# A mixture-of-experts stage rebuilt: gate rows gathered with the tokens, the sum done by the scatter, products issued early

## The chip, the cores and the metric

One core of a Trainium2 chip runs the whole program. The metric is the device time in microseconds, the median of several runs; one further execution is recorded by the hardware profiler, and all rows below come from it. Engines: TensorE (PE; weight loads are PEld), VectorE (DVE), ScalarE (ACT), GpSimd (POOL) and the DMA queue of SyncE (SP). GpSimd issues the indirect DMAs, which gather or scatter rows by an index in SBUF.

## What is computed

A block with two halves over x of shape (2, 2048, 256), all float32. The first half is a layer norm, linear attention with 16 heads and a gated residual; the change touches none of it but a store. The second is a top-2 mixture of 8 experts:

```python
h = layernorm(x) * (1 + cb) + sb
probs = softmax(h @ router_w.T)                 # 4096 tokens, 8 experts
topw, topi = top_k(probs, 2); topw /= topw.sum() + 1e-6
# each expert keeps the 640 tokens with the largest weight
g, u = disp[e] @ wg[e], disp[e] @ wu[e]         # (640,256) @ (256,1024)
eo = (silu(g) * u) @ wd[e]                      # (640,1024) @ (1024,256)
out = x + gb[b] * scatter_add(eo * weight)      # gb: a gate row of 256 for each of 2 batches
```

## The kernel before

**Precision.** Each float32 operand of the expert products is split into a high half (rounded to fp32r) and a low half (the rest), and each product is three TensorE passes: high x high, high x low, low x high. ScalarE casts the high half of the weights (`split_high`, L644), GpSimd subtracts it for the low half (`split_low`, L508, one block f of 768 columns at a time).

**Attention part** (to about 237 us). SP stores the layer-normed rows h2 to `h2_rows` in DRAM and x with its attention to `out`.

**Routing** (to about 309 us). `choose` finds the two experts and the weights `wgt`, in two parts, and builds `val`: the weight where an expert is chosen, weight minus one elsewhere. A search on the bits of `val` finds each expert's threshold, then slots are counted. For each expert a one-hot product on TensorE (`look`) turns slots into token numbers.

**Experts.** E = 8 experts run one after the other, e = 0 to 7. Each has 640 tokens in CT = 5 tiles of 128, and 1024 hidden units in FC = 8 blocks f of 128. For block f, `gate_up(f)` on TensorE makes gate and up products in two halves h of 320 tokens (12 products each); ScalarE takes the SiLU (L673), VectorE multiplies by up (L1089, here "hidden(f,h)"), ScalarE casts the high half (L677), VectorE subtracts for the low half (L1092). `down(f)` adds 15 products into the banks 4 to 6. The order on TensorE is gate_up(0), gate_up(1), down(0), gate_up(2), down(1) and so on to gate_up(7), down(6), the look-up of expert e+2, down(7). gate_up(f) in half h waits for hidden(f-1,h), since that frees its bank. At f = 4, 5 and 6 the gathered rows of the next expert are transposed.

Around this run, in each engine's own order:

- VectorE: at the start of e, `weigh(e-1)` (L1070) multiplies the five result tiles by `gw`; `combine` (L1078) adds the gathered old rows `xo` of `out`. At f = 0 to 4 it builds `gw` (L1101), gate row times token weight, with ScalarE's share from L664. At f = 1 `find_tokens(e+1)` writes the index tiles; at f = 2 to 6 `describe_*` prepares the look-up of e+2.
- GpSimd: the scatter of e-1 (each tile waits for `combine`), the splits of f = 6 and 7 of e, the gathers of `xg` for e+1 (five, 1 KB rows of `h2_rows`), the gathers of `xo` for e (five, from `out`), then the splits of f = 0 to 5 of e+1. A program-wide rule is that accesses of `out` follow each other, by the semaphore `sc_d` of landed scatters.
- SP: loads the weights of the next experts in two halves, each when both splits of the blocks before it are done.

Of the kernel before, what the change touches and what calls it, by code (L numbers as in the profile page):

```python
# [26 lines left out]
N = B * T  # L27
# [20 lines left out]
XF = 4  # L48
# [72 lines left out]
def build_program(nc, x, w_qkv, w_out, router, wg, wu, wd, c, wmod, rope, consts, out):  # L121
# [3 lines left out]
    h2_rows = nc.dram_tensor("h2_rows", (N, D), F32, kind="Internal").ap()  # L125
    h2_t = h2_rows.rearrange("(n p) d -> n p d", p=P)
# [3 lines left out]
    with ExitStack() as ctx:  # L130
# [40 lines left out]
        val = sb("val", [P, NT, E])  # L171
# [23 lines left out]
        far = sb("far", [P, CT])  # L195
        g_idx = [sb(f"g_idx{i}", [P, CT], I32) for i in range(2)]
        s_idx = [sb(f"s_idx{i}", [P, CT], I32) for i in range(2)]
        w_slot = sb("w_slot", [P, 3, CT])
        w_b = [sb(f"w_b{i}", [P, B, CT]) for i in range(2)]
# [53 lines left out]
        xg = sb("xg", [P, CT, D])  # L253
# [6 lines left out]
        gw0 = sb("gw0", [P, D])  # L260
        gw = sb("gw", [P, CT, D])
        xo, yo = sb("xo", [P, CT, D]), sb("yo", [P, CT, D])
# [38 lines left out]
        raw_a, raw_b, sp_h, sp_l = sem("raw_a"), sem("raw_b"), sem("sp_h"), sem("sp_l")  # L301
# [3 lines left out]
        y_tile, wb_l, wb_d = sem("y_tile"), sem("wb_l"), sem("wb_d")  # L305
        gw0_d, gw_d, xo_d, ym_d, yo_d, sc_d = (sem(n) for n in ("gw0_d", "gw_d", "xo_d", "ym_d", "yo_d", "sc_d"))
# [7 lines left out]
        def _(sp):  # L314
# [69 lines left out]
            steps(sp, step, ATT)  # L384

# [22 lines left out]
        def _(pool):  # L408
# [81 lines left out]
            pool.wait_ge(r_dve, 3)  # L490
# [23 lines left out]
            def gather(rows, dst, idx, done):  # L514
                for a in range(CT):
                    nc.gpsimd.indirect_dma_start(  # L516
                        out=dst[:, a, :], out_offset=None, in_=rows,
                        in_offset=bass.IndirectOffsetOnAxis(ap=idx[:, a:a + 1], axis=0))\
                        .then_inc(done[a // 2] if isinstance(done, list) else done, 16)

            for i in range(2):
                pool.wait_ge(st_h2[i], NT // 2 * 16)
                pool.wait_ge(st_x2[i], NT // 2 * 16)
            pool.wait_ge(idx_d, 1)
            gather(h2_rows, xg, g_idx[0], ga_d)

            def expert(e, par, last):
                for f in (0, 1):
                    split_low(e, FC - 2 + f, e * FC + FC - 2 + f)
                if last < 1:  # L530
                    wait_apart(pool, idx_d, e + 2, apart)
                    wait_apart(pool, trx_d, e * XG + XG, apart)
                    gather(h2_rows, xg, g_idx[1 - par], ga_d)
                wait_apart(pool, sc_d, e * CT * 16 + 16, apart)
                gather(out_rows, xo, g_idx[par], xo_d)
                if last < 1:
                    for f in range(FC - 2):
                        split_low(e + 1, f, e * FC + FC + f)
                for a in range(CT):
                    wait_apart(pool, yo_d, e * CT + a + 1, apart)  # L540
                    nc.gpsimd.indirect_dma_start(  # L541
                        out=out_rows, out_offset=bass.IndirectOffsetOnAxis(ap=s_idx[par][:, a:a + 1], axis=0),
                        in_=yo[:, a, :], in_offset=None, bounds_check=N - 1, oob_is_err=False).then_inc(sc_d, 16)

            with pool.Fori(0, (E - 2) // 2) as k:
                expert(k * 2, 0, 0)
                expert(k * 2 + 1, 1, 0)
            expert(E - 2, 0, 0.5)
            expert(E - 1, 1, 1)
# [4 lines left out]
        def _(act):  # L554
# [104 lines left out]
            def expert(e, par, last):  # L659
                def gate_weight(a):  # L660
                    wait(act, wb_d, e + 1)
                    if a:
                        wait(act, gw_d, e * CT + a)
                    nc.scalar.activation(gw0[:, :], mod_all[:, 0, 3, :], ACT.Copy, scale=w_b[par][:, 0, a:a + 1])\  # L664
                        .then_inc(gw0_d, 1)

                for f in range(FC):
                    for h in range(2):
                        i = e * 2 * FC + 2 * f + h
                        wait(act, gu_d, i + 1)  # L670
                        if f:
# [3 lines left out]
                        if f >= 2:  # L675
                            wait(act, dn_d, e * FC + f - 1)
                        nc.scalar.copy(hid_h[f % 2][:, h * HCAP:(h + 1) * HCAP], hid[h][:, :]).then_inc(hh_d, 1)  # L677
                    if last < 1 and XF <= f < XF + XG:
# [4 lines left out]
                    elif last < 1:  # L683
                        split_high(e + 1, f - 2, e * FC + FC + f - 2)
                    if f < CT:
                        gate_weight(f)

            with act.Fori(0, (E - 2) // 2) as k:
                expert(k * 2, 0, 0)
                expert(k * 2 + 1, 1, 0)  # L690
            expert(E - 2, 0, 0.5)
            expert(E - 1, 1, 1)


        @block.vector
        def _(dve):
# [70 lines left out]
            def choose(lo, hi):  # L767
# [31 lines left out]
                TT(X[1], X[4], b8(Y[6]), ALU.mult)  # L799
# [127 lines left out]
            def place_masks(part):  # L927
# [3 lines left out]
                for k, op in enumerate((ALU.is_gt, ALU.is_equal)):  # L931
                    ins = TT(mask2[:, k, lo:hi, :].rearrange("p e n -> p n e"), val[:, :, lo:hi], tb, op)
# [86 lines left out]
            def find_tokens(e, par):  # L1019

                lk = chained(fin_l, e * 3)
# [375 lines left out]
```

## Time and profile before

| | |
|---|---|
| Median of 3 runs | 758.37 us (756.48 to 760.09) |
| Span of the profiled execution | 752.9 us |
| Span of it in experts 0 to 7 | 309.3 to 752.9 us |
| Busy: PE, DVE, POOL, ACT | 601.8, 523.0, 417.9, 334.2 us |

The profiled span leaves out what lies around it: the median of the runs is 5.5 us above. In a timeline row the columns are the start (us from the span's start), the time taken (us), the engine, the line of the kernel and the operation, then output and inputs, how many instructions are merged, and in brackets how long the engine was idle before it and what ended that. A row of the chain has start, duration and what the time went to.

### The profile page before, as it was taken

To read this page: it belongs to the slowest core of one execution; us is meant where nothing else is said; L and a number is where in the kernel's file an instruction comes from. 1 tells how busy PE (TensorE), PEld (TensorE's weight loads), DVE (VectorE), ACT (ScalarE), POOL (GpSimd) and SP (SyncE) were. 2 spreads that over 40 slices of the span, in tenths; PEclk is the share of its full clock that TensorE was granted. 3 is DMA by queue.
4 is the path that set the end of the run, shared out by engine and by line. 5 is a ranking of instruction groups with operands and counts; after the bars stand their busy time and mean duration, and the time that the engine had idled before them with its cause. 6 is when DMAs were issued, how large, how long until landed. Compare 5 with 4: busy or idle time off the path is not lost.

```text
span 752.9 us, 14123 instructions
## 1 busy us (share of the span) xinstructions
PE 601.8 (80%) x4041; PEld 557.5 (74%) x4041; DVE 523.0 (69%) x1366; ACT 334.2 (44%) x759; POOL 417.9 (55%) x538
## 2 busy tenths in 40 slices
PE   3999789998982002788989989979979979979993
PEld 2677678886761001788978979969969969979993
DVE  2688899996777877665766766757747757736743
ACT  4577677875443000344334424424434425335440
POOL 6689658786773601254474475474473473563612
PEclk9999999999995555698999999999988999989997
DMA  4322268435550200041241341251242152150101
GB/s 123 109 70 70 90 204 248 151 116 179 182 176 17 84 0 11 26 138 36 87 150 34 97 150 46 84 153 50 69 153 82 37 154 81 39 155 1 46 26 35
DMA packets 80467, 70.68 MB, mean 94 GB/s; under 512 B 8604, under 2 KB 75558, under 8 KB 80424
## 3 DMA queue, kind: packets, MB, share of 16 engines
q1 hardware_dynamic: 74632, 54.44, 23.7%
q0 software_dynamic: 5792, 15.74, 6.5%
q8 instruction: 18, 0.29, 0.2%
q14 instruction: 25, 0.20, 0.1%
HBM read 52.32 MB, written 17.83 MB: 93 GB/s over the span
## 4 chain that ended last, share of the span: by engine, by line
PE 41%; DVE 24%; issue 13%; ACT 5%; POOL 2%; DVEq 1%; DMA 1%; ACTq 0%; SPq 0%; POOLq 0%
PE bank L1329 22%; PE bank L1341 12%; DVE gw L1101 3%; DVE feat L855 2%; PE bank L1287 2%; DVE hit L908 2%; ACT w_h L644 2%; DVE hid L1089 2%; DVE x L874 2%; PE bank L1301 2%; ACT act_g L673 1%; DVE st L876 1%; PE bank L1242 1%; DVE cand L919 1%; DVE yo L1078 1%
## 5 line engine op out<-in xcount | busy, mean ns | idle before, releaser
L1329 PE MATMUL bank<-xT_h,w_h 128*128 128x320 f32 x512 | 166.4, 325 | 20.7 <-DVE hid L1089 18.8
L508 POOL TENSOR_TENSOR w_l<-w_raw,w_h 128x768 fp32r<-128x768 f32 x64 | 120.5, 1901 | 111.2 <-ACT w_h L644 111.1
L1329 PE MATMUL bank<-xT_l,w_h 128*128 128x320 f32 x512 | 164.7, 322 | 2.1 <-issue 2.1
L1329 PE MATMUL bank<-xT_h,w_l 128*128 128x320 f32 x512 | 164.2, 321 | 1.8 <-issue 1.8
L677 ACT CAST hid_h<-hid 128x320 fp32r<-128x320 f32 x128 | 58.9, 460 | 136.4 <-DVE hid L1089 114.0
L1329 PEld LDWEIGHTS bank<-xT_h,w_h 128*128 128x128 f32 x512 | 102.5, 200 | 22.5 <-DVE hid L1089 16.1
L1092 DVE TENSOR_TENSOR hid_l<-hid,hid_h 128x320 fp32r<-128x320 f32 x128 | 67.0, 524 | 70.0 <-ACT hid_h L677 58.5
L673 ACT ACTIVATE act_g<-bank 128x320 f32<-128x320 f32 x128 | 55.4, 432 | 114.3 <-remote 58.3
L1089 DVE TENSOR_TENSOR hid<-act_g,bank 128x320 f32<-128x320 f32 x128 | 61.6, 481 | 61.0 <-ACT act_g L673 60.5
L1329 PEld LDWEIGHTS bank<-xT_l,w_h 128*128 128x128 f32 x512 | 102.5, 200 | 2.0 <-issue 2.0
L1329 PEld LDWEIGHTS bank<-xT_h,w_l 128*128 128x128 f32 x512 | 101.8, 199 | 2.3 <-issue 2.3
L1341 PE MATMUL bank<-w_h,hid_h 128*128 128x256 f32 x320 | 96.4, 301 | 4.2 <-issue 3.5
L1341 PE MATMUL bank<-w_h,hid_l 128*128 128x256 f32 x320 | 94.7, 296 | 3.6 <-issue 3.6
L1341 PE MATMUL bank<-w_l,hid_h 128*128 128x256 f32 x320 | 94.6, 296 | 0.5 <-issue 0.5
L541 POOL DMA_INDIRECT out<-yo,s_idx x40 | 40.0, 1001 | 72.9 <-DVE yo L1078 65.6
L516 POOL DMA_INDIRECT xg<-h_rows,g_idx x40 | 39.2, 980 | 66.3 <-DVE s_idx L1032 44.7
L1101 DVE SCALAR_TENSOR_TENSOR gw<-mod_all,w_b,gw 128x256 f32<-128x256 f32 x40 | 58.6, 1466 | 18.2 <-ACT gw L664 11.0
L1341 PEld LDWEIGHTS bank<-w_h,hid_h 128*128 128x128 f32 x320 | 64.6, 202 | 6.1 <-issue 6.0
L1341 PEld LDWEIGHTS bank<-w_h,hid_l 128*128 128x128 f32 x320 | 64.8, 202 | 3.8 <-issue 3.8
L1341 PEld LDWEIGHTS bank<-w_l,hid_h 128*128 128x128 f32 x320 | 65.2, 204 | 2.2 <-issue 2.2
L480 POOL TENSOR_TENSOR rot<-rot_a,rot_b 128x512 f32<-128x512 f32 x32 | 46.8, 1463 | 15.3 <-DVE rot_b L839 15.3
L1150 PE MATMUL bank<-wqkv_h,hT_h 128*128 128x256 f32 (+1 forms) x128 | 47.3, 369 | 8.3 <-DVE hT_l L846 4.5
(199 smaller groups left out, 1321.7 us busy)
## 6 DMA issues: line engine op xcount, KB each, us to landing
w_raw<-wg SPq DMA_DIRECT2D x32, 256.0 KB, 3.1
w_raw<-wu SPq DMA_DIRECT2D x32, 256.0 KB, 4.4
w_raw<-wd SPq DMA_DIRECT2D x16, 512.0 KB, 5.9
x_in<-x SPq DMA_DIRECT2D x32, 128.0 KB, 2.0
q_store<-qT SPq DMA_DIRECT2D x32, 128.0 KB, 1.7
q_in<-q_store SPq DMA_DIRECT2D x32, 128.0 KB, 2.1
x_re<-x SPq DMA_DIRECT2D x32, 128.0 KB, 2.1
out<-x SPq DMA_DIRECT2D x32, 128.0 KB, 2.0
```

The source lines that it names most:

```text
L480: nc.gpsimd.tensor_tensor(rot[s.par(0)][:, :], rot_a[:, :], rot_b[:, :], ALU.add).then_inc(rope_d, 1)
L508: nc.gpsimd.tensor_tensor(w_l[:, f, :], w_raw[:, f, :], w_h[:, f, :].bitcast(F32), ALU.subtract)\
L516: nc.gpsimd.indirect_dma_start(out=dst[:, a, :], out_offset=None, in_=rows, in_offset=bass.IndirectOffsetOnAxis(ap=idx[:, a:a + 1], axis=0))\
L541: nc.gpsimd.indirect_dma_start(out=out_rows, out_offset=bass.IndirectOffsetOnAxis(ap=s_idx[par][:, a:a + 1], axis=0), in_=yo[:, a, :], in_ ...
L673: nc.scalar.activation(act_g[h][:, :], bank[2 * h][:, 0:HCAP], ACT.Silu).then_inc(silu_d, 1)
L677: nc.scalar.copy(hid_h[f % 2][:, h * HCAP:(h + 1) * HCAP], hid[h][:, :]).then_inc(hh_d, 1)
L1089: V.tensor_tensor(hid[h][:, :], act_g[h][:, :], bank[2 * h + 1][:, 0:HCAP], ALU.mult)\
L1092: V.tensor_tensor(hid_l[f % 2][:, h * HCAP:(h + 1) * HCAP], hid[h][:, :], hid_h[f % 2][:, h * HCAP:(h + 1) * HCAP].bitcast(F32), ALU.subtr ...
L1101: V.scalar_tensor_tensor(gw[:, f, :], mod_all[:, 1, 3, :], w_b[par][:, 1, f:f + 1], gw0[:, :], ALU.mult, ALU.add).then_inc(gw_d, 1)
L1150: ins = MM(out, x[j][:, k, :], w[i][:, k, cols], start=n == 0, stop=n == 3 * KC - 1)
L1329: last = MM(bank[2 * h + m][:, 0:HCAP], W[i][:, f, at:at + P], XT[j][:, k, cols], start=n == 0, stop=n == 3 * KC - 1)
L1341: last = MM(bank[4 + a // 2][:, a % 2 * D:(a % 2 + 1) * D], (hid_h, hid_l)[j][f % 2][:, a * P:(a + 1) * P], W[i][:, f, 4 * P:], start=f == ...
```

## The change

- `h2_rows` becomes twice as wide: a row is the normed token and, behind it, the gate row of its batch. SP writes the gate rows for all tokens with two DMAs behind the attention part. A gather now brings both, 2 KB a row, into `xg`, which is doubled.
- `gw`, ScalarE's scaling and VectorE's gate product go. `weigh` becomes one product of result, token weight and gathered gate row, and stands in block f = 0 in two parts.
- The gathers of `xo` and `combine` go; the scatter adds to `out` in the DMA. Empty slots point to token 0 with weight zero.
- `s_idx` is one tile. `find_targets(e)` at f = 3 on VectorE copies the indices once scatter e-1 has landed.
- GpSimd's order becomes: splits 6 and 7 of e, gather of e+1, scatter of e-1, splits 0 to 5 of e+1.
- TensorE issues gate_up(e+1,0) ahead of down(e,7), and gate_up(e+1,1) behind it; the look-up stands ahead of down(6). On VectorE, find_tokens and the describe steps stand between a hidden product and its low half.
- The `val` array goes; the search works on `wgt`.

```diff
-    h2_rows = nc.dram_tensor("h2_rows", (N, D), F32, kind="Internal").ap()
+    h2_rows = nc.dram_tensor("h2_rows", (N, 2 * D), F32, kind="Internal").ap()
+    gate_t = h2_rows[:, D:].rearrange("(b n p) d -> b p n d", b=B, p=P)
...
             steps(sp, step, ATT)
+            sp.wait_ge(ld_all, 3 * B * 16)
+            for b in range(B):
+                sp.dma_start(gate_t[b], mod_all[:, b, 3, :].unsqueeze(1).to_broadcast([P, TB, D])).then_inc(st_gate, 16)
...
+            def scatter(e):
+                wait_apart(pool, sc_d, e * CT * 16 + 16, apart)
+                for a in range(CT):
+                    wait_apart(pool, ym_d, e * CT + a + 1, apart)
+                    nc.gpsimd.indirect_dma_start(
+                        out=out_rows, out_offset=bass.IndirectOffsetOnAxis(ap=s_idx[:, a:a + 1], axis=0),
+                        in_=yo[:, a, :], in_offset=None, compute_op=ALU.add).then_inc(sc_d, 16)
...
+            def expert(e, par, first=False, last=False):
                 for f in (0, 1):
                     split_low(e, FC - 2 + f, e * FC + FC - 2 + f)
-                if last < 1:
+                if not last:
+                    if not first:
+                        wait_apart(pool, ym_d, e * CT, apart)
                     wait_apart(pool, idx_d, e + 2, apart)
-                    wait_apart(pool, trx_d, e * XG + XG, apart)
-                    gather(h2_rows, xg, g_idx[1 - par], ga_d)
-                wait_apart(pool, sc_d, e * CT * 16 + 16, apart)
-                gather(out_rows, xo, g_idx[par], xo_d)
-                if last < 1:
+                    gather(e + 1, 1 - par)
+                if not first:
+                    scatter(e - 1)
+                if not last:
                     for f in range(FC - 2):
                         split_low(e + 1, f, e * FC + FC + f)
-                for a in range(CT):
-                    wait_apart(pool, yo_d, e * CT + a + 1, apart)
...
-                    if f < CT:
-                        gate_weight(f)
...
-                link(TT(X[7], X[3], X[4], ALU.add))
-                link(TT(wgt[:, lo:hi, :], X[0], X[1], ALU.add))
-                V.tensor_scalar(X[5], X[7], -1.0, None, ALU.add).then_inc(r_dve, 1)
-                dve.wait_ge(r_dve, 1 + 2 * part)
-                TT(val[:, lo:hi, :], wgt[:, lo:hi, :], X[5], ALU.add).then_inc(r_dve, 1)
+                TT(wgt[:, lo:hi, :], X[0], X[1], ALU.add).then_inc(r_dve, 1)
...
+            def find_targets(e, par):
+                wait(dve, sc_d, e * CT * 16 + 16)
+                V.tensor_copy(s_idx[:, :], g_idx[par][:, :])
...
+                    V.scalar_tensor_tensor(yo[:, a, :], bank[4 + a // 2][:, a % 2 * D:(a % 2 + 1) * D],
+                                           w_slot[par][:, a:a + 1], xg[par][:, a, D:], ALU.mult, ALU.mult).then_inc(ym_d, 1)
...
+                for f in range(FC):
+                    hidden(f, 0)
+                    if f == 0 and not first:
+                        weigh(e - 1, 1 - par, 0, 2)
+                    if f == 1 and not last:
+                        find_tokens(e + 1, 1 - par)
+                    if f == 2 and ahead:
+                        describe_tiles(e + 2)
+                    if f == 3:
+                        find_targets(e, par)
+                    if f in (3, 4) and ahead:
+                        describe_facts(e + 2, f - 3)
+                    if f == 5 and ahead:
+                        describe_rows(e + 2, 0)
+                    hidden_low(f, 0)
+                    hidden(f, 1)
+                    if f == 0 and not first:
+                        weigh(e - 1, 1 - par, 2)
...
+            def expert(e, par, last=False, ahead=True):
+                for f in range(2, FC):
+                    gate_up(e, par, f)
+                    if not last and XF <= f < XF + XG:
+                        transpose_x(e + 1, 1 - par, f - XF)
+                    if f == FC - 1 and ahead:
+                        wait(pe, xl_d, e * XG + 2 * XG)
+                        look(e + 2)
+                    down(e, f - 1)
+                if not last:
+                    gate_up(e + 1, 1 - par, 0)
+                down(e, FC - 1)
+                if not last:
+                    gate_up(e + 1, 1 - par, 1)
+                    down(e + 1, 0)
```

## Rows read from the trace of the kernel before

**Rows 1.** The page: busy us of each engine, share of the span, instructions.
```profile
PE 601.8 (80%) x4041; PEld 557.5 (74%) x4041; DVE 523.0 (69%) x1366; ACT 334.2 (44%) x759; POOL 417.9 (55%) x538
```
**Rows 2.** Who waited for whom on PE: total us, times, longest.
```profile
PE bank L1329 <- DVE hid L1089: 18.8, 9, 2.9
```
**Rows 3.** The chain that ended last: start us, us, what.
```profile
336.00 1.68 issue
...
341.92 3.15 PE bank L1341 x14
345.06 4.83 PE bank L1329 x24
...
366.88 1.77 PE bank L1329 x12
...
422.10 1.78 PE bank L1329 x12
...
438.90 5.31 PE bank L1329 x24
...
467.89 3.52 PE bank L1329 x24
471.41 1.79 PE bank L1341 x15
473.21 2.03 PE bank L1287 x32
...
696.86 1.78 PE bank L1329 x12
```
**Rows 4.** Timeline of VectorE in expert 2.
```profile
432.85 4.44 DVE L1101 SCALAR_TENSOR_TENSOR gw<-mod_all,w_b,gw 128x256 f32<-128x256 f32 x1 [0.65 <-ACT gw L664]
...
442.13 0.48 DVE L1101 SCALAR_TENSOR_TENSOR gw<-mod_all,w_b,gw 128x256 f32<-128x256 f32 x1 [0.65 <-ACT gw L664]
...
447.58 0.57 DVE L991 TENSOR_TENSOR facts<-vals,in_tile 128x400 bf16<-128x400 f32 x1
```
**Rows 5.** Timeline of GpSimd in experts 2 and 5.
```profile
433.35 3.65 POOL L508 TENSOR_TENSOR w_l<-w_raw,w_h 128x768 fp32r<-128x768 f32 x2
439.38 0.99 POOL L516 DMA_INDIRECT xg<-h_rows,g_idx  x1 [2.38 <-issue]
...
451.12 0.95 POOL L516 DMA_INDIRECT xo<-out,g_idx  x1 [0.30 <-issue]
...
605.98 0.99 POOL L516 DMA_INDIRECT xg<-h_rows,g_idx  x1 [2.30 <-issue]
```
**Rows 6.** Timeline of ScalarE in experts 2 and 5.
```profile
431.58 0.83 ACT L644 CAST w_h<-w_raw 128x768 fp32r<-128x768 f32 x1
...
453.74 0.44 ACT L673 ACTIVATE act_g<-bank 128x320 f32<-128x320 f32 x1 [6.59 <-remote]
...
620.26 0.44 ACT L673 ACTIVATE act_g<-bank 128x320 f32<-128x320 f32 x1 [6.66 <-remote]
```
**Rows 7.** Busy us by stretch; last three: granted clock, DMA share, GB/s.
```profile
226.00:245.00 19.00, 4.28 (x18) 3.08 (x18) 14.98 (x61) 7.00 (x15) 6.06 (x11) 0.56 0.04 14
440.00:442.00 2.00, 2.00 (x10) 2.00 (x9) 0.95 (x2) 1.51 (x4) 1.39 (x3) 0.50 0.89 242
```
**Rows 8.** Timeline of all engines: the first gathers.
```profile
299.19 0.96 POOL L516 DMA_INDIRECT xg<-h_rows,g_idx  x1 [0.30 <-issue]
...
301.96 1.11 PE L1301 MATMUL bank<-const_sb,xg 128*128 128x128 f32 x4 [2.69 <-DMA xg<-h_rows,g_idx]
```
**Rows 9.** Timeline of VectorE at the end of choose.
```profile
242.12 0.21 DVE L804 TENSOR_TENSOR val<-wgt,big 128x48 f32<-128x48 f32 x1
```
**Rows 10.** Timeline at the end: first and last scatter.
```profile
742.76 1.01 POOL L541 DMA_INDIRECT out<-yo,s_idx  x1 [24.50 <-DVE yo L1078]
...
748.16 0.97 POOL L541 DMA_INDIRECT out<-yo,s_idx  x1 [0.31 <-issue]
```

More of the change, by code:

```diff
@@ L657, in _, with expert @@
                 x_high(0, 0, g, bk=g)
[L659 to L665, printed above, removed]
+            def expert(e, par, first=False, last=False):
                 for f in range(FC):
@@ L670, in expert @@
                         wait(act, gu_d, i + 1)
-                        if f:
+                        if f or not first:
                             wait(act, hid_d, i - 1)
@@ L1097, in expert @@
                     if not last and XF <= f < XF + XG:
                         x_low(e + 1, 1 - par, f - XF)
-                    if f < CT:
-                        wait(dve, gw0_d, e * CT + f + 1)
-                        V.scalar_tensor_tensor(gw[:, f, :], mod_all[:, 1, 3, :], w_b[par][:, 1, f:f + 1], gw0[:, :],
-                                               ALU.mult, ALU.add).then_inc(gw_d, 1)
-                    if f == 1 and not last:
-                        find_tokens(e + 1, 1 - par)
@@ L1105, in expert @@
-                    if f == FC - 1 and not last:
-                        find_weights(e + 1, 1 - par)
-                    if ahead:
-                        if f == 2:
-                            describe_tiles(e + 2)
-                        if f in (3, 4):
-                            describe_facts(e + 2, f - 3)
-                        for part in {3: (0,), 5: (1,), 6: (2, 3)}.get(f, ()):
-                            describe_rows(e + 2, part)
+                    if f == 6 and ahead:
+                        describe_rows(e + 2, 3)
@@ L1256, in _ @@
             steps(pe, step, ATT)
-            pe.wait_ge(r_dve, 4)
-            flat = val[:, :, :].rearrange("p n e -> p (n e)")
+            pe.wait_ge(r_dve, 2)
+            flat = wgt[:, :, :].rearrange("p n e -> p (n e)")
             for k in range(2):
@@ new lines, in gate_up @@
+                wait(pe, sp_l, e * FC + f + 1)
+                if f == 0:
+                    wait(pe, xl_d, e * XG + XG)
+                for h in range(2):
+                    if f or not first:
+                        wait(pe, hid_d, e * 2 * FC + 2 * f + h - 1)
+                    cols = slice(h * HCAP, (h + 1) * HCAP)
+                    for m in range(2):
+                        n = 0
+                        for k in range(KC):
+                            for i, j in PASSES:
+                                at = (2 * m + k) * P
+                                last = MM(bank[2 * h + m][:, 0:HCAP], W[i][:, f, at:at + P], XT[j][:, k, cols],
+                                          start=n == 0, stop=n == 3 * KC - 1)
+                                n += 1
+                    last.then_inc(gu_d, 1)
@@ new lines, in down @@
+            def down(e, f):
+                wait(pe, hh_d, e * 2 * FC + 2 * f + 2)
+                wait(pe, hl_d, e * 2 * FC + 2 * f + 2)
+                if f == 0:
+                    wait(pe, ym_d, e * CT)
+                for a in range(CT):
+                    for n, (i, j) in enumerate(PASSES):
+                        last = MM(bank[4 + a // 2][:, a % 2 * D:(a % 2 + 1) * D],
+                                  (hid_h, hid_l)[j][f % 2][:, a * P:(a + 1) * P], (w_h, w_l)[i][:, f, 4 * P:],
+                                  start=f == 0 and n == 0 and a % 2 == 0, stop=f == FC - 1 and n == 2,
+                                  skip_group_check=True)
+                    if f == FC - 1 and a % 2 == 1:
+                        last.then_inc(y_tile, 1)
+                last.then_inc(dn_d, 1)
@@ L1360, in _ @@
+            gate_up(0, 0, 0, first=True)
+            gate_up(0, 0, 1)
+            down(0, 0)
             with pe.Fori(0, (E - 2) // 2) as k:
-                expert(k * 2, 0, 0)
-                expert(k * 2 + 1, 1, 0)
-            expert(E - 2, 0, 0.5)
-            expert(E - 1, 1, 1)
+                expert(k * 2, 0)
+                expert(k * 2 + 1, 1)
+            expert(E - 2, 0, ahead=False)
+            expert(E - 1, 1, last=True, ahead=False)
 def kernel(L0_attn_x, L0_attn_W_qkv, L0_attn_W_out, L0_ffn_router_w, L0_ffn_wg, L0_ffn_wu, L0_ffn_wd, L0_c, L0_wmod):
```

188 lines of the change are left out of this document (65 added, 123 removed).

## The prediction

> **What bounds the kernel now.** I read the page's busy shares first: TensorE works 80% of the span and nothing else comes near it [rows 1]. The chain of work then gives the clock of the expert stage. Expert 1 opens its first gate/up products at 366.88 and expert 7 at 696.86, so a full expert takes 330.0 / 6 = 55.0 us [rows 3]. What TensorE needs when nothing holds it is in the same view: 3.52 us for 24 gate/up products, 1.79 us for 15 down products, 2.03 us for the look-up [rows 3]. Ten transposes, of which four take 1.11 us while the clock is at half [rows 8], are 1.4 us at full clock at most; I take 1.1, since their ends overlap the next products. That is 8 x 5.31 + 2.03 + 1.1 = 45.7 us. So 9.3 us per expert are lost, in two places.
>
> First, the VectorE product that builds the gate weight for f=1 takes 4.44 us where 0.48 us is usual; it starts at 432.85 and ends when GpSimd's two back-to-back low-half splits end (433.35 + 3.65 = 437.0) [rows 4, 5]. Behind it on VectorE stand find_tokens and the next hidden product, and TensorE waits for that product: 18.8 us in 9 waits over the span, about 2.65 us an expert [rows 2]. After the wait 24 products take 5.31 us, not 3.52, at a granted clock of 0.50 (1.2 of 2.4 GHz): 1.8 us more [rows 3, 7].
>
> Second, at f=4 every engine but GpSimd stands still. ScalarE's SiLU starts at 453.74 after 6.59 us without work, and at 620.26 in expert 5 after 6.66 [rows 6]; in expert 0 TensorE waits and crawls from 336.00 to 341.92 [rows 3]. It ends 14.3 us after the first of ten back-to-back indirect DMAs (five of xg, five of xo) begins, in expert 2 (439.38 to 453.74) as in expert 5 (605.98 to 620.26), and 2.6 us after the last one begins at 451.12 [rows 5, 6]. I read it as something that this burst of ten does, not as the transposes. It costs some 3 us net an expert, with a second stretch at half clock behind it.
>
> **The change part by part.**
> *Gate weights gone.* Five ScalarE scalings (0.5 us each) and five VectorE gate products leave each expert, the 4.44 us one among them. The 2.65 + 1.8 us of the first loss go.
>
> *xo gathers and combine gone, gate rows gathered.* GpSimd issues 5 gathers and 5 scatters an expert instead of 10 and 5: 5 x 1.25 = 6.3 us less on its queue. But gather and scatter now stand in one row, so there is still a burst of ten. The new yo product is VectorE work of 256 columns like the gate product it replaces (0.48 us [rows 4]), five an expert: 5 x 0.45 us once they overlap, bounds 0.40 and 0.48. I take a gather of 2 KB rows at the issue time of one of 1 KB (0.95 us; lower bound the same, upper bound twice that), since it has the same 128 rows.
>
> *The add in the scatter.* Its landing is not in this trace. Lower bound: a plain gather issued at 299.19 releases TensorE at 301.96, 2.8 us [rows 8]. Upper bound: the last scatter is issued at 748.16 and the span ends at 752.9, 4.7 us with the program's end in it [rows 10]. The DMAs are not full at that point, so I take 3.2 us, nearer to the gather.
>
> *The new wait.* find_targets(e) stands on VectorE at f=3, behind hidden(3,0), and waits until scatter(e-1) has landed. Behind it wait the low half of (3,0) and hidden(3,1), and for that TensorE's second half of gate_up(4). When does scatter(e-1) land? Count from T, the end of the first half of gate_up(e,0):
> - TensorE without stalls: other half 1.76, down(e-1,7) 1.8, gate_up(1) 3.52, so gate_up(1) ends at T+7.1; gate_up(2) runs 8.9 to 12.4, gate_up(3) 14.2 to 17.7, and the first half of gate_up(4) ends at T+21.3.
> - VectorE: hidden(0,0), two yo products, low half, hidden(0,1) (0.4 to 0.5 us each, the yo products held until down(e-1,7) reaches them) to T+4.4, three yo products to T+5.7, low half, hidden(1,0) to T+6.5. ScalarE's cast for split 6 follows hidden(0,1) by 0.5 us and takes 0.83 [rows 6], so GpSimd's split 6 (half of 3.65, with its end 1.85 us) starts near T+5.7, a tie with the low half. If VectorE wins it, find_tokens meets the split and ends at T+8.5; hidden(1,1) ends at 9.4, the cast for split 7 at 10.7, split 7 at T+12.6. If it loses, everything is 0.8 us later; I add 0.3.
> - The burst: 0.15 us, then 11.74 us between the first and the tenth issue [rows 5], plus 0.15 since scatters go every 1.28 us: the last issue is at T+24.65. Landed at T+27.85.
> - find_targets 0.2, describe_facts 0.5 (0.57 alone [rows 4]), low half 0.45, hidden(3,1) 0.5: TensorE goes on at T+29.5. It stood still for 8 us.
>
> The rest of the expert is 45.7 - 21.3 = 24.4 us, and 2.1 us for the restart at half clock (1.8 was paid after 2.6 us idle; at least that). Period: 29.5 + 24.4 + 2.1 + 0.3 = 56.3 us against 55.0. The stall of the burst lies wholly inside the new wait. Six experts (1 to 6): **+7.8 us**.
>
> The Trainium skill states the rule behind the first loss (SBUF — State Buffer, Who interferes with whom): a VectorE instruction with two SBUF inputs and a GpSimd instruction that reads SBUF exclude each other for the whole instruction. The trace agrees: the gate product, both inputs in SBUF, ended 0.3 us after the splits. By the rule and by the row the sum is the same; by the rule the yo product, with an operand in PSUM, is never held.
>
> *Expert 0* has no wait in find_targets and a burst of five only, which in expert 7 of the kernel before brought no standstill. Gone: the late hidden product (0.6, in the total of [rows 2], and 24 products in 3.79 instead of 3.52), the standstill of 5.9 us less the 1.0 us of work done in it, and what half clock cost behind it: 14 down products 3.15 instead of 1.68 us, gate_up 4.83 instead of 3.52 [rows 3]. Sum **-8.6 us**.
>
> *Expert 7* loses its late product (1.9 us with what follows) but its scatter(6), five issues behind split 7, lands at T+12.75+5.1+3.2 = T+21.1 and gives TensorE 0.7 us of waiting: **-1.2 us**.
>
> *Routing.* The val array goes. In the second part its two last instructions end at 242.33 [rows 9], 0.55 us after wgt would; in the first part it is 1.0 us more, which counts only if the logits are there; together -1.3 us taken (0.6 to 1.6). find_tokens(0) is 0.3 us shorter and the first gathers of 2 KB rows land about 0.3 us later: **-1.3 us**.
>
> *Gate store.* Two DMAs write 4 MB on SP behind the last h2 store. From 226 to 245 the DMAs run at 14 GB/s [rows 7], and the first gather reads these rows after 297; at the 200 to 300 GB/s of busy stretches it is 14 to 20 us. It costs nothing; without that cover it would be those 14 to 20 us.
>
> *Early first products.* gate_up(e+1,0) stands ahead of down(e,7). TensorE did not wait at that place before (the chain runs on at 473.21 and later), so it gives nothing itself; it gives the yo products cover. describe_rows(3) has 2 us to spare before the earlier look-up.
>
> *Tail.* Without combine the first scatter leaves 0.5 us earlier after the last product; five issues go at the same pace (742.76 to 748.16 [rows 10]); the add lands 0.4 to 0.8 us later: **+0.3 us**.
>
> Sum against the profiled span of 752.9: +7.8 - 8.6 - 1.2 - 1.3 + 0.3 = -3.0, a span of 749.9. The median of the runs stands 5.5 us above the span (758.37), so **755.3 us**.
>
> **The rivals.** All turn on the period, and each microsecond in it is six in the time.
> - *The adding scatter is slow (other side).* If it is issued or lands later than a plain one by 1.5 us or more in each expert, by reading the destination before writing it, the wait at f=3 grows by that: taken as 2.7 us an expert it gives 6 x 2.7 + 0.7 in expert 7 = 17 us more, 772 us. It decides from 0.5 us beyond my 3.2: 6 x 0.5 takes the 3.0 us of gain. For it: no row has such a DMA, and find_targets waits for all five. Against: the DMAs are nearly idle then.
> - *The skill's price.* The Trainium skill (DMA: Bandwidth & Descriptors, Latency and other measured facts) puts HBM access at 0.2 us on average and 2 us at high load; one more such trip would give, as an estimate, 0 to 10 us above my time, and this trace has no row for it.
> - *The chain is shorter than I count.* Split 7 a microsecond earlier (find_tokens not caught by split 6), landing at 2.8, restart at 1.7: period 54.5, and 755.3 - 6 x 1.8 = 744 us. For it: the ScalarE queue is 2.5 us lighter. Against: the ten issues are serial and nothing shortens them.
> - *The standstill belongs to the transposes or to the weight load*, not to the burst. Then it stays in expert 0 and comes again after the new wait: 3 to 5 us in seven experts, 780 to 790 us. Against: experts 2 and 5 are freed at the same distance from the burst to 0.1 us, and e = 7, which has a burst of five, shows none.
>
> **How the numbers follow.** Forecast with its own range 748 to 763: 0.45. Slow adding scatter: 0.24. Shorter chain: 0.19. Standstill stays: 0.07. The rest, 0.05, is a slower gather of 2 KB rows (780). Range 742 to 778. A measurement here tells about 0.5% (3.8 us) from no change. Faster by more: half of the forecast's cases and all of the shorter chain, 0.42. Within: the other half less the few of its range that end above, and the mildest slow scatters, 0.26. Slower: 0.32.
>
> **What would show it.** Right: no VectorE product over 2 us at f=1; VectorE idle before find_targets' copy for some 10 us in experts 1 to 6, ended by the scatter's landing; TensorE idle about 8 us before the second half of gate_up(4) there, and none of it in expert 0; period 56.3. Wrong: scatters spaced over 1.3 us or landing over 4 us; down(e,0) or gate_up(2) late because the low half lost to split 6; a standstill at the transposes after the new wait; half clock for longer than some 4 us after each stop.

## The result: 770.9 us, slower than before

| | before | after |
|---|---|---|
| Median of 4 runs | 758.57 us (756.48 to 760.09) | 770.92 us (767.01 to 773.58) |
| Ratio | | 1.0175 (95% interval 1.0132 to 1.0218) |
| Span of the profiled execution | 752.9 us | 770.1 us |
| First gate/up products of experts 0, 1, 6, 7 | 309.3, 366.7, 643.4, 696.7 | 310.1, 357.2, 648.8, 704.5 |
| End of the last product | 741.9 | 754.1 |
| Busy PE, DVE, POOL, ACT | 601.8, 523.0, 417.9, 334.2 | 595.9, 442.3, 400.2, 320.8 |

Every engine has less to do than before, and the kernel is 1.75% slower. The page of the kernel after, busy row (the counterpart of [rows 1]) and the groups that the argument needs:

```profile
PE 595.9 (77%) x4041; PEld 553.7 (72%) x4041; DVE 442.3 (57%) x1248; ACT 320.8 (42%) x717; POOL 400.2 (52%) x498
...
L1323 PE MATMUL bank<-xT_h,w_h 128*128 128x320 f32 x512 | 167.6, 327 | 54.6 <-DVE hid L1073 42.8
...
L528 POOL DMA_INDIRECT out<-yo,s_idx x40 | 62.7, 1568 | 39.0 <-DVE yo L1063 27.3
L518 POOL DMA_INDIRECT xg<-h_rows,g_idx x40 | 39.2, 980 | 50.6 <-DVE g_idx L1023 39.8
```

The late hidden product cost TensorE 18.8 us before [rows 2] and 42.8 us now. The gather of a 2 KB row takes 0.98 us to issue, as one of 1 KB did; the adding scatter 1.57 us, where the plain one took 0.97 [rows 10].

Expert 2 after, which begins at 415.78. GpSimd's timeline, then VectorE's, TensorE's and ScalarE's (the counterparts of [rows 4 to 6]):

```profile
427.71 1.85 POOL L509 TENSOR_TENSOR w_l<-w_raw,w_h 128x768 fp32r<-128x768 f32 x1 [2.53 <-ACT w_h L652]
429.72 1.01 POOL L518 DMA_INDIRECT xg<-h_rows,g_idx  x1
...
436.10 1.63 POOL L528 DMA_INDIRECT out<-yo,s_idx  x1 [0.30 <-issue]
438.03 1.58 POOL L528 DMA_INDIRECT out<-yo,s_idx  x1 [0.30 <-issue]
...
443.65 1.55 POOL L528 DMA_INDIRECT out<-yo,s_idx  x1 [0.30 <-issue]
```

```profile
447.54 0.17 DVE L1028 COPY s_idx<-g_idx 128x5 int32<-128x5 int32 x1 [7.52 <-DMA out<-yo,s_idx]
447.72 0.58 DVE L986 TENSOR_TENSOR facts<-vals,in_tile 128x400 bf16<-128x400 f32 x1
448.21 0.48 DVE L1078 TENSOR_TENSOR hid_l<-hid,hid_h 128x320 fp32r<-128x320 f32 x1
448.62 0.48 DVE L1073 TENSOR_TENSOR hid<-act_g,bank 128x320 f32<-128x320 f32 x1
```

```profile
449.15 0.64 PE L1323 MATMUL bank<-xT_h,w_h 128*128 128x320 f32 x1 [5.96 <-DVE hid L1073]
```

```profile
439.05 0.44 ACT L674 ACTIVATE act_g<-bank 128x320 f32<-128x320 f32 x1 [6.55 <-remote]
```

The ten issues run from 429.72 to 443.65. VectorE's copy of the indices, 0.17 us long, stands from 440 to 447.54 and is released by the last scatter. The copies as a group (the view of one tile):

```profile
who waited for it (us, times):
  DVE s_idx L1028: 55.3, 7
```

TensorE goes on at 449.15, at half clock (windows; the clock is the column behind POOL):

```profile
443.00:449.10 6.10, 0.19 (x1) 0.00 (x0) 1.55 (x4) 0.00 (x0) 3.74 (x3) 0.50 0.39 45
449.10:452.60 3.50, 3.45 (x13) 3.41 (x14) 2.40 (x4) 1.99 (x4) 1.82 (x1) 0.50 0.01 2
452.60:457.00 4.40, 4.40 (x30) 4.40 (x29) 2.12 (x5) 2.12 (x4) 1.50 (x1) 0.81 0.00 0
```

The old stop of ScalarE is still there ("remote", 6.55 us), but in front of the SiLU of block 3. It ends before the copy begins to wait: TensorE stands 2.44 us for the stop and 5.96 us for the copy, and since the copy waits for the landing, at 447.5, the stop adds nothing to the time. In expert 7, the chain:

```profile
725.58 3.77 DMA out<-yo,s_idx
729.35 0.02 issue
729.37 0.04 DVE s_idx L1028
729.41 0.04 issue
729.46 0.48 DVE hid_l L1078
729.94 0.41 DVE hid L1073
```

### The profile page after: what moved, and what is told of

It reads as the page before. It is cut to its first block, busy times and chain, and to the rows that moved or that the text cites. A ratio compares the mean times of both kernels' runs of the same rounds, so it can differ in the third digit from the quotient of the medians.

```text
span 770.1 us, 13880 instructions
## 1 busy us (share of the span) xinstructions
PE 595.9 (77%) x4041; PEld 553.7 (72%) x4041; DVE 442.3 (57%) x1248; ACT 320.8 (42%) x717; POOL 400.2 (52%) x498
## 4 chain that ended last, share of the span: by engine, by line
issue 32%; POOL 19%; DVE 18%; PE 13%; DMA 3%; ACT 1%; DVEq 1%; SPq 1%; POOLq 0%; ACTq 0%
POOL w_l L509 9%; POOL out L528 7%; PE bank L1323 6%; PE bank L1335 3%; POOL xg L518 2%; DVE feat L850 2%; DVE hit L903 2%; DVE x L869 1%; DMA out<-yo,s_idx 1%; DVE st L871 1%; PE bank L1238 1%; DVE cand L914 1%; DVE den_r L856 1%; DMA x_in<-x 1%; DVE hid L1073 1%
## 5 line engine op out<-in xcount | busy, mean ns | idle before, releaser
L509 POOL TENSOR_TENSOR w_l<-w_raw,w_h 128x768 fp32r<-128x768 f32 x64 | 123.4, 1932 | 204.7 <-ACT w_h L652 204.7
L1323 PE MATMUL bank<-xT_h,w_h 128*128 128x320 f32 x512 | 167.6, 327 | 54.6 <-DVE hid L1073 42.8
L1323 PE MATMUL bank<-xT_h,w_l 128*128 128x320 f32 x512 | 166.2, 325 | 0.0
L1335 PE MATMUL bank<-w_h,hid_h 128*128 128x256 f32 x320 | 94.4, 295 | 0.4 <-DVE hid_l L1078 0.4
L1335 PE MATMUL bank<-w_h,hid_l 128*128 128x256 f32 x320 | 91.5, 286 | 1.2 <-issue 1.1
L1335 PE MATMUL bank<-w_l,hid_h 128*128 128x256 f32 x320 | 91.3, 285 | 0.2 <-issue 0.2
L1078 DVE TENSOR_TENSOR hid_l<-hid,hid_h 128x320 fp32r<-128x320 f32 x128 | 63.5, 496 | 35.5 <-ACT hid_h L678 35.5
L528 POOL DMA_INDIRECT out<-yo,s_idx x40 | 62.7, 1568 | 39.0 <-DVE yo L1063 27.3
L1335 PEld LDWEIGHTS bank<-w_h,hid_l 128*128 128x128 f32 x320 | 62.5, 195 | 0.8 <-issue 0.8
L1335 PEld LDWEIGHTS bank<-w_l,hid_h 128*128 128x128 f32 x320 | 62.2, 194 | 1.1 <-issue 1.0
L652 ACT CAST w_h<-w_raw 128x768 fp32r<-128x768 f32 x64 | 52.9, 833 | 0.0
```

The costliest lines, as they stand in the source:

```text
L509: nc.gpsimd.tensor_tensor(w_l[:, f, :], w_raw[:, f, :], w_h[:, f, :].bitcast(F32), ALU.subtract)\
L528: nc.gpsimd.indirect_dma_start(out=out_rows, out_offset=bass.IndirectOffsetOnAxis(ap=s_idx[:, a:a + 1], axis=0), in_=yo[:, a, :], in_offse ...
L652: nc.scalar.copy(w_h[:, f, :], w_raw[:, f, :]).then_inc(sp_h, 1)
L1078: V.tensor_tensor(hid_l[f % 2][:, h * HCAP:(h + 1) * HCAP], hid[h][:, :], hid_h[f % 2][:, h * HCAP:(h + 1) * HCAP].bitcast(F32), ALU.subtr ...
L1323: last = MM(bank[2 * h + m][:, 0:HCAP], W[i][:, f, at:at + P], XT[j][:, k, cols], start=n == 0, stop=n == 3 * KC - 1)
L1335: last = MM(bank[4 + a // 2][:, a % 2 * D:(a % 2 + 1) * D], (hid_h, hid_l)[j][f % 2][:, a * P:(a + 1) * P], (w_h, w_l)[i][:, f, 4 * P:], s ...
```

## The experiments

Twelve kernels, each beside runs of the kernel before on the same chip. That kernel's median was 757.8, 754.0 and 753.7 us in the three groups of four, so between groups the ratios to it are what to compare. The three kernels with an overwriting scatter leave out the add to the old rows of `out` and so compute something else; they are there to price the add.

| kernel | median us | ratio to before (95%) | period of experts 1 to 5, us |
|---|---|---|---|
| after | 770.9 | 1.0175 (1.0132 to 1.0218) | 58.2 to 58.6 |
| two tiles of targets | 725.9 | 0.9575 (0.9540 to 0.9609) | 51.3 to 53.0 |
| scatter that overwrites | 740.0 | 0.9764 (0.9720 to 0.9808) | 53.4 to 54.3 |
| targets found at f = 6 | 727.7 | 0.9613 (0.9575 to 0.9652) | 51.4 to 51.5 |
| two tiles, overwriting scatter | 738.6 | 0.9734 (0.9694 to 0.9774) | 54.2 to 54.5 |
| two tiles, load held | 730.5 | 0.9688 (0.9663 to 0.9713) | 51.2 to 53.9 |
| two tiles, scatters apart | 694.8 | 0.9210 (0.9187 to 0.9233) | 46.6 to 46.7 |
| two tiles, all DMAs apart | **689.8** | 0.9150 (0.9126 to 0.9173) | 45.7 to 45.8 |
| two tiles, late products | 731.8 | 0.9675 (0.9621 to 0.9728) | 52.9 to 54.3 |
| all apart, overwriting scatter | 689.3 | 0.9154 (0.9128 to 0.9181) | 45.7 to 45.8 |
| before, gathers apart | 726.3 | 0.9655 (0.9618 to 0.9692) | 51.4 to 52.3 |
| all apart, late products | 690.7 | 0.9180 (0.9150 to 0.9211) | 45.7 to 45.8 |
| all apart, bounds check | 689.8 | 0.9160 (0.9134 to 0.9187) | 45.7 to 45.8 |

A period is the time from the first gate/up product of one expert to that of the next.

### The wait of find_targets: two tiles, or a later place

```diff
-        s_idx = sb("s_idx", [P, CT], I32)
+        s_idx = [sb(f"s_idx{i}", [P, CT], I32) for i in range(2)]
...
-                wait(dve, sc_d, e * CT * 16 + 16)
-                V.tensor_copy(s_idx[:, :], g_idx[par][:, :])
+                V.tensor_copy(s_idx[par][:, :], g_idx[par][:, :])
```

> The changed kernel with two tiles of scatter targets, so that find_targets(e) waits for nothing and the rest is as it was. Theory (the late landing of the adding scatter reaches TensorE only through this copy): TensorE's 42.8 us of waiting at the second half of gate_up(4) goes, and the stretch at half clock behind it, some 2 us in each of seven experts. Against that stands the stop of ScalarE inside the burst, now hidden behind the wait, which comes back in front of TensorE at 2 to 3 us net in experts 1 to 6. Period 58.3 - 8.3 + 2.5 to 3 = 52.5 to 53, time 732 to 740 us against 770.9. Rival (the burst of ten DMAs holds the engines up by itself, and the copy only happened to stand there): TensorE waits as long for the next SiLU, period over 57, time 760 to 771.

```diff
-                    if f == 3:
-                        find_targets(e, par)
...
-                    if f == 6 and ahead:
-                        describe_rows(e + 2, 3)
+                    if f == 6:
+                        if ahead:
+                            describe_rows(e + 2, 3)
+                        find_targets(e, par)
```

> The changed kernel with find_targets moved from f = 3 to the end of f = 6, still one tile, still waiting for the scatter. The scatter lands some 32 us after gate_up(e,0) begins and block 6 of VectorE comes 12 us or more after that. Theory (place of the wait decides): as with two tiles of targets, within 2 us of its time, 732 to 741 us. Rival (VectorE is too late anyway, or the scatter lands later once nothing holds the experts back): the wait shows again at f = 6, time 745 us or more.

Measured 725.9 and 727.7 us: 45 and 43 us less than the changed kernel, more than I expected, and nearly the same by either edit. So the wait at f = 3 was more than the whole loss, and the place of 0.17 us of work decides some 6% of the time. With the later place a period fell by 7 us in experts 1 to 5, where I had expected 5.5; with two tiles by 7 in experts 1 to 3 and by 5 in 4 and 5.

But it did not fall to the 45.7 us that TensorE needs. Expert 2 with two tiles, which begins at 405.78, ScalarE's, VectorE's and GpSimd's timelines:

```profile
429.84 0.44 ACT L674 ACTIVATE act_g<-bank 128x320 f32<-128x320 f32 x1 [7.34 <-remote]
```

```profile
434.52 4.80 DVE L986 TENSOR_TENSOR facts<-vals,in_tile 128x400 bf16<-128x400 f32 x1
439.25 0.48 DVE L1077 TENSOR_TENSOR hid_l<-hid,hid_h 128x320 fp32r<-128x320 f32 x1
```

```profile
433.64 1.55 POOL L528 DMA_INDIRECT out<-yo,s_idx  x1 [0.30 <-issue]
434.63 4.25 POOL L509 TENSOR_TENSOR w_l<-w_raw,w_h 128x768 fp32r<-128x768 f32 x2
```

Two things remain. ScalarE's SiLU stands 7.34 us: the increment of TensorE's semaphore that frees it is recorded at 429.81, for products that ended near 423.5. TensorE's own products keep their pace until 426.6 and then come with gaps. And a facts product of VectorE takes 4.80 us instead of 0.57, until two low-half splits, which had piled up behind the ten DMAs, are done. The next runs take these apart.

### The add in the scatter

```diff
-                        in_=yo[:, a, :], in_offset=None, compute_op=ALU.add).then_inc(sc_d, 16)
+                        in_=yo[:, a, :], in_offset=None).then_inc(sc_d, 16)
```

> The changed kernel with a scatter that overwrites: the add to the old rows of out is left out, nothing else. Theory (the add makes each scatter dearer to issue and later to land): spacing of the issues back from 1.86 to 1.28 us, landing from 3.8 to 2.4 to 2.8 us, so the wait of find_targets is 4 x 0.58 + 1.2 = 3.5 us shorter in experts 1 to 7 and the tail about 3.5 us shorter: 770.9 - 8 x 3.5 = 743 us. Rival (the add costs nothing; issue and landing are late since these DMAs stand behind five gathers of 2 KB rows): spacing and landing stay, 768 to 773 us.

> Two tiles of targets and the overwriting scatter together; the add is left out. Theory (once nothing waits for the landing, the price of the add counts only at the end of the program): 3.5 to 5 us below the kernel with two tiles of targets. Rival (the longer burst holds GpSimd's splits or ScalarE up in every expert): each of six experts is also 1 to 2.5 us shorter, 10 to 18 us below it.

Alone the edit gives 740.0 us, near the 743 of the theory, but by a larger term than it had: VectorE's wait for the landing falls from 55.3 to 22.5 us over seven experts, 4.7 an expert and not 3.5. The scatters are issued 1.28 us apart again. The last issue to the last increment of `sc_d` takes 2.40 us at the end of this run, and 3.73 us with the add in the changed kernel.

With two tiles both expectations fell: without the add the kernel is not 4 us or more faster but 12.7 us slower (738.6 against 725.9). ScalarE's timeline of that kernel, expert 2 from 412.37:

```profile
436.45 0.44 ACT L674 ACTIVATE act_g<-bank 128x320 f32<-128x320 f32 x1 [7.37 <-remote]
437.51 0.46 ACT L678 CAST hid_h<-hid 128x320 fp32r<-128x320 f32 x1 [0.63 <-issue]
440.77 0.44 ACT L674 ACTIVATE act_g<-bank 128x320 f32<-128x320 f32 x1 [2.79 <-remote]
```

The stop has grown a second part of 2.79 us, where the scatter with the add has none, or one of up to 1.5, in experts 1 to 5. More of the loss is in the clock. These are the windows from the first expert product to the last, without the add and then with it:

```profile
309.89:724.10 414.21, 388.12 (x2758) 380.18 (x2758) 202.25 (x441) 165.54 (x336) 177.23 (x128) 0.93 0.26 83
307.35:709.00 401.65, 378.50 (x2758) 371.93 (x2758) 225.60 (x441) 163.63 (x336) 198.64 (x128) 0.97 0.33 86
```

The same products keep TensorE busy 9.6 us longer, at a granted clock of 0.93 instead of 0.97, and it is idle only 2.9 us more. Why quicker scatters lead to longer or more stops is open; that they crowd the transfers is a guess that no run here separates. With all DMAs apart (below) the same edit changes nothing:

> Two tiles of targets and DMAs in small groups (689.8 us before, 0.915 of the kernel before), with the overwriting scatter; the add is left out. Theory (in this arrangement the add is paid at the end of the program alone): issue 5 x 0.58 and landing 1.3 us less there, GpSimd's drain behind it perhaps 2.5 us longer, as with the overwriting scatter in a row: 685.5 to 689 us, periods of 45.7 us as with the add. Rival (the longer issue takes GpSimd's time in every expert): periods shorter by 0.5 us or more, 683 us or less. A third way, by the pair in which the add was the faster: quicker scatters crowd the transfers again, over 692 us.

689.3 us, 0.3 above the theory's range, ratio 0.9154 beside 0.9150, periods equal. Issue and landing at the end are shorter, but GpSimd's drain behind them is longer: 6.7 us, where it is 4.1 with the add and 2.0 in the kernel before. In an arrangement in which nobody waits for the landing, the add is free.

### The stop: weight load or burst

```diff
+                wait(sp, sc_d, e * CT * 16 + 16)
                 load_weights(e + 1, FC // 2, raw_b)
```

> The kernel with two tiles of targets (725.9 us), in which SyncE holds the weight load that starts beside the burst until scatter e-1 has landed, in experts 1 to 6. In that kernel the increment by which TensorE frees ScalarE comes some 6 us late (429.81 for products that ended near 423.5) while load, gathers and scatters are in flight. Theory A (the overlap of the load with the burst delays it): no ScalarE wait over 2 us at f = 3 and 4 in experts 1 to 6, two stops of 2 to 3 us net fewer; against it the load is late for the cast of block 4 at f = 6, 0 to 3 us an expert: 708 to 722 us, and the stop gone in the trace. Theory B (ten indirect DMAs in a row do it, load or no load): the stop of 6 to 7 us stays at the same distance from the first gather, 726 to 742 us.

The stop shrank and the time did not: 730.5 us, and by the ratios (0.9688 beside 0.9575) the kernel is about 1% slower than with the load in its old place. So neither theory came out whole. In expert 3 of that kernel (from 461.00), ScalarE:

```profile
481.32 0.44 ACT L675 ACTIVATE act_g<-bank 128x320 f32<-128x320 f32 x1 [3.60 <-PE bank L1323]
```

and later VectorE and GpSimd:

```profile
490.00 6.30 DVE L1078 TENSOR_TENSOR hid_l<-hid,hid_h 128x320 fp32r<-128x320 f32 x1 [0.53 <-ACT hid_h L679]
```

```profile
489.95 5.99 POOL L510 TENSOR_TENSOR w_l<-w_raw,w_h 128x768 fp32r<-128x768 f32 x3
```

In each of experts 1 to 6 the stop is 1.5 to 3.7 us shorter than with the load beside it (1.8 to 4.3 us, where it was 3.3 to 7.3). But a stop needs no load. The kernel before had its stop of expert 2 from 447.15 to 453.74, and in that time its load had landed. All DMA traffic from 446 to 454 (queue, packets, MB, share of the 16 engines):

```profile
q0 software_dynamic: 299, 0.81, 35.1%
```

These are gathers alone; the load runs on q1. Nor does the load fix the size of the stop: in the kernel with two tiles and late products, below, it is in place beside ten indirect DMAs, and the stop is 4.3 to 4.4 us in experts 1 to 5. How much of the stop is the load's is therefore not shown.

The few microseconds won ran straight into the pile: three splits back to back hold a low half for 6.30 us, and TensorE stands for 3.2 us, to 497.0. The late load itself, which I had priced at 0 to 3 us, was not what it met. The Trainium skill (SBUF — State Buffer, Who interferes with whom) states the exclusion that the prediction cited: a VectorE instruction with two SBUF inputs contends with a GpSimd instruction that reads SBUF, over a shared port pair that is an exclusive lock. The trace agrees: the low half, both inputs in SBUF, ends 0.36 us after the third split.

### The DMAs apart

GpSimd's order with two tiles of targets. The edit shown is that of the second kernel, in which at most three stand in a row; the conditions for the first and last expert and the old loop of splits are left out of it. The first kernel keeps the five gathers together and sets the scatters apart in twos:

```diff
-                    gather(e + 1, 1 - par)
...
-                    scatter(e - 1, 1 - par)
...
+                    gather(e + 1, 1 - par, 0, 2)
+                    split_low(e + 1, 0, e * FC + FC + 0)
+                    gather(e + 1, 1 - par, 2, 4)
+                    split_low(e + 1, 1, e * FC + FC + 1)
+                    gather(e + 1, 1 - par, 4, CT)
+                    scatter(e - 1, 1 - par, 0, 1)
+                    split_low(e + 1, 2, e * FC + FC + 2)
+                    scatter(e - 1, 1 - par, 1, 3)
+                    split_low(e + 1, 3, e * FC + FC + 3)
+                    scatter(e - 1, 1 - par, 3, CT)
+                    split_low(e + 1, 4, e * FC + FC + 4)
+                    split_low(e + 1, 5, e * FC + FC + 5)
```

> Two tiles of targets; GpSimd issues the five gathers together, but the scatters two, two and one with a low-half split in front of each group. Load as it was. Theory A (load and gathers together do it): the first stop stays, 722 to 728 us. Theory B (the number of indirect DMAs in a row): five in a row as in expert 0, whose stop hardly reaches TensorE: 2 to 3 us an expert less, 708 to 715 us.

> Two tiles of targets; no more than two or three indirect DMAs of GpSimd in a row, gathers and scatters alike, with splits between the groups. Load as it was. Theory A (the load beside any gathers): the DMAs are less full at one time, so the stop shrinks by a third and the time is 716 to 724 us. Theory B (number in a row): no stop, 706 to 713 us. Against both, the last gathers land some 4 us later, which the transposes at f = 5 and 6 could feel by up to 1 us.

694.8 and 689.8 us, better than either theory had it, since I had priced the stop alone and the pile of splits went with it. In the first kernel, five gathers in a row beside the load still leave ScalarE standing 4.4 us in experts 1 to 5, of which TensorE feels 0.6 to 0.8 us. The page of the second and its windows in expert 3 (from 445.48):

```profile
PE 570.9 (83%) x4041; PEld 533.6 (78%) x4041; DVE 435.0 (63%) x1248; ACT 321.2 (47%) x717; POOL 400.8 (58%) x498
```

```profile
459.00:463.00 4.00, 4.00 (x32) 4.00 (x31) 2.44 (x8) 2.10 (x4) 2.98 (x4) 1.00 0.51 148
463.00:467.00 4.00, 4.00 (x32) 4.00 (x31) 2.41 (x6) 2.17 (x5) 3.06 (x3) 1.00 0.95 300
467.00:471.00 4.00, 4.00 (x31) 3.99 (x30) 1.65 (x5) 1.69 (x4) 3.11 (x3) 1.00 0.60 207
```

TensorE is busy throughout at a granted clock of 1.00, a period is 45.7 us (what the prediction counted as TensorE's need, though its terms add up to 45.6), and no VectorE instruction in the expert stage takes over 1.5 us. The DMAs are 95% busy at 463 to 467 with the load in flight, so 4 us of full DMAs don't make a stop, and the stop of the kernel before stood at 35%. GpSimd issued two gathers in a row there, not five and five more DMAs.

The same grouping in the kernel before, its ten gathers in the same pattern:

> The kernel before, with one edit: its ten gathers of an expert stand in groups of one to three with the low-half splits of blocks 0 to 4 between them. It asks how much of the 68 us between the kernel before and the best one is the grouping alone. Theory (the row of ten makes TensorE's increments late and piles the splits up behind it): the stop at f = 4 (6.6 us without work, 3 to 4 us net with its half clock) goes in experts 0 to 6, the gate product held by the two splits of f = 6 and 7 stays: 758 - 7 x 4 = 725 to 735 us. Rival (the stop has another cause in this kernel): 750 us or more. If 700 us or less, the rest of the change is worth nothing.

726.3 us, within the theory. The stop is gone, and the gate product is held as ever (VectorE's timeline):

```profile
423.73 4.45 DVE L1116 SCALAR_TENSOR_TENSOR gw<-mod_all,w_b,gw 128x256 f32<-128x256 f32 x1 [0.65 <-ACT gw L679]
```

So of the ratio of 0.915 the grouping alone is worth 0.9655, and the change without its wait brings the rest: 51.4 us a period become 45.7.

### Early first products and the end of the program

```diff
-                if not last:
-                    gate_up(e + 1, 1 - par, 0)
                 down(e, FC - 1)
                 if not last:
+                    gate_up(e + 1, 1 - par, 0)
                     gate_up(e + 1, 1 - par, 1)
```

> Two tiles of targets, with gate_up(e+1,0) back behind down(e,7) on TensorE. Theory (the early first products give only cover to the yo products): without them TensorE waits for the first SiLU, hidden product and cast of the next expert at the seam only where those are late; VectorE's first yo products come no earlier, so gate_up(e+1,1) waits up to 1 us for the hidden product: 726 to 733 us. Rival (worth nothing): within 2 us of 725.9. Rival (worth much, since TensorE otherwise stands still for SiLU, hidden product and cast before down(e+1,0)): 735 us or more.

> Two tiles of targets and DMAs in small groups, with gate_up(e+1,0) back behind down(e,7). With ten DMAs in a row this cost 6 us at the median, but the products at the seam ran without a gap there, so I put the 6 us down to the stop and the held low half that fell at another place. Theory: the seam itself is worth nothing, 689 to 691.5 us, 0.915 of the kernel before. Rival (TensorE waits at the seam): 5 us or more over that.

731.8 us with the burst, 690.7 with the DMAs apart: ratios 0.9675 against 0.9575, and 0.9180 against 0.9150, whose intervals overlap. So early products are worth about 1 us at most in themselves, near the nothing of the prediction. The 6 us beside the burst (its four runs go from 725.6 to 733.7) are not lost at the seam, where TensorE's products run without a gap. VectorE's low half is held for 6.3 to 6.4 us in experts 1 to 5 there, where with early products a facts product is held for 4.8 to 4.95 in experts 1 to 4:

```profile
438.11 6.41 DVE L1077 TENSOR_TENSOR hid_l<-hid,hid_h 128x320 fp32r<-128x320 f32 x1 [0.53 <-ACT hid_h L678]
```

> Two tiles of targets and DMAs in small groups; the scatter gets the bounds check of the kernel before, with the add kept. Behind the last landing GpSimd drains for 2.0 us in the kernel before and for 4.2 us here. Theory (the drain follows the kind of the scatter): the check brings the 2.0 us back, issue spacing unchanged, 687 to 688.5 us. Rival (the drain follows something else): drain of 4.2 us, time 689 to 690.5 us.

689.8 us and a drain of 4.1 us: the theory fell. Why the drain is 2.0, 4.1 or 6.7 us is open; a bounds check in the adding scatter isn't it. The overwriting scatter with the check, as the kernel before has it, was not run in the new kernel.

## Why the prediction was wrong

It gave 755.3 us with chances of 0.42 for faster and 0.32 for slower; the time is 770.9, inside the range of 742 to 778, and it is the rival "the adding scatter is slow" that happened (forecast at 772, chance 0.24). That its 772 comes so near is partly luck: it took 2.7 us more an expert, where 1.9 to 2.3 are measured in experts 1 to 5, and had no term for the tail. Span against predicted span: 770.1 - 749.9 = 20.2 us. In order:

- **Periods of experts 1 to 6: +9.6 us** (347.4 against 337.8). The step that failed is the burst: "11.74 us between the first and the tenth issue, plus 0.15 since scatters go every 1.28 us". They go every 1.86 us, and the ten take 13.93 us: +2.0 an expert. The landing, 3.2 us taken, is 3.8 to 3.9: +0.6. The burst began 0.6 us earlier than counted. The periods are 1.9 to 2.3 us over the forecast in experts 1 to 5; expert 6, where nothing is described ahead, had 0.5 us less than forecast. The rest of the chain held: 1.6 us from landing to TensorE (1.65 predicted), 25.1 us from there to the next expert in expert 2 (25.0), VectorE's low half before the split as chosen.
- **Expert 7: +3.8 us.** The same scatter lands 2 us later than "T+21.1"; TensorE waits 2.67 us instead of 0.7, and runs at half clock behind it, which the term left out: 12 products take 3.27 us.
- **Tail: +4.7 us** (16.0 us from the last product against 11.3). "Five issues go at the same pace" failed: against the kernel before they take 2.0 us more, the landing 1.3 (0.4 to 0.8 was forecast) and GpSimd's drain 2.2 (nothing was forecast); the first scatter leaves 0.55 us earlier, as predicted.
- **Start of expert 0: +2.1 us.** No error of a step that can be shown: twelve profiled executions with the same code up to there start it between 307.35 and 310.13.
- **Expert 0: right.** 47.02 us measured, 47.1 predicted in the same count: five DMAs in a row left only a short stop.
- Against these 20.2 us stand 4.7 us between span and median: 5.5 before, 0.8 after. In every execution on record the time stands 1.7 to 3.1 us above the span of that same execution (772.49 against 770.1 here), so most of the 5.5 us that the prediction added was the difference between two executions of the kernel before.

The landing had a lower and an upper bound; the *issue* of the adding scatter had none. Its pace was taken from the plain one [rows 10], in the burst and in the tail. Eight times 4 x 0.58 us is 18.6 us of issue alone, seven of them in front of a wait. The rival named both ("issued or lands later"), with its time, but its chance was set as if only the landing were open. As to the sentence on the Trainium skill (DMA: Bandwidth & Descriptors, Latency and other measured facts): the add's landing is 3.73 - 2.40 = 1.33 us later, between its 0.2 and 2 us for a trip to HBM. The trace agrees in size, and no run shows that it is such a trip.

The reading of the stop was right as far as it went. It belongs to the burst and not to the transposes: it moved to the SiLU of block 3 with the burst, and went from both kernels when the DMAs were set apart. The weight load, which the prediction gave to a rival together with the transposes, is not its cause in the kernel before, where it had landed; in the new kernel, where it runs beside the burst, taking it away shortens the stop.

Not settled: why an increment of TensorE's semaphore comes up to 6 us late while indirect DMAs are in flight. Shown is only that their number in a row, their pace, the load beside them and the place of TensorE's products each change it.

## What to carry to other kernels

An instruction of 0.2 us that waits for a DMA holds all that stands behind it on its engine: give it a second buffer, or place it where the DMA has long landed, before anything is tuned around it. When an operation gets a new mode, such as an add in a scatter, its issue needs bounds of its own as much as its landing, multiplied by how many are issued in a row ahead of the wait. A row of ten indirect DMAs on GpSimd cost twice here, by late increments and by the work that piles up behind it and then holds VectorE; two or three at a time between GpSimd's other work cost nothing, and were worth 27 us in the kernel before without another change.

## What the runs showed of the hardware that was not expected

- The adding scatter of 128 rows of 1 KB is issued every 1.86 us and lands 3.73 us after the last issue begins; the plain one every 1.28 us and 2.40 us.
- In a row of ten beside a load, the slower scatter was the faster kernel by 12.7 us (725.9 against 738.6), of which 9.6 us were TensorE's products, at a granted clock of 0.97 against 0.93; with the DMAs apart the two are equal.
- While such a row is in flight, a semaphore increment of TensorE is recorded 6 us after its products ended (429.81 for 423.5), though the products behind them keep their pace for another 3 us. In the kernel before the same stop, 6.59 us, stood with the DMAs 35% busy and no load in flight.
- GpSimd's drain at the end of the program took 2.0 us behind the scatters of the kernel before, 4.1 behind adding ones and 6.7 behind overwriting ones of the new kernel.
